# A decoder block on one core: ring sizes, quantiser instructions, bank choice and issue orders changed together

## The reference

```python
x = layernorm(x + attention(x))        # 16 heads of 32, causal, softmax in f32, biases
x = layernorm(x + cross(x, ctx))       # q, k from ctx (256 wide); A = softmax(q k^T) over 512; out = x @ A^T
x = layernorm(x + ffn(x))              # the line below

xq = clip(round(s * r), -128, 127) / s          # r = (x - mean) / sqrt(var + 1e-8), s = 127 / max|r| per row
ffn = (silu(xq @ sign(W_g).T) * (xq @ sign(W_u).T)) @ sign(W_d).T     # hidden width 2048
```

## Time and profile before

| what | value |
|---|---|
| median of three runs | 581.6 us |
| the profiled execution: its time, its span | 582.68 us, 580.9 us |
| TensorE (PE) busy | 550.0 us, 95% |
| VectorE (DVE) busy | 478.7 us, 82% |
| ScalarE (ACT) busy | 420.7 us, 72% |
| GpSimd (POOL) busy | 381.3 us, 66% |
| granted TensorE clock, mean | 0.989 |

### The profile page before, as it was taken

One profiled execution on the slowest core, in us unless ns is written; L12 is line 12 of the kernel. 1 busy time (PEld: TensorE's weight loads), 2 busy tenths in 40 slices (PEclk: granted clock), 3 DMA queues, 4 the chain that ended last, 5 costly groups with the idle time before them and its releaser, 6 DMA issues.

```text
span 580.9 us, 14215 instructions
## 1 busy us (share of the span) xinstructions
PE 550.0 (95%) x5324; PEld 356.2 (61%) x5324; DVE 478.7 (82%) x1252; ACT 420.7 (72%) x789; POOL 381.3 (66%) x409
## 2 busy tenths in 40 slices
...
GB/s 303 304 332 186 272 244 261 81 55 91 137 65 183 138 120 181 191 173 93 90 110 160 136 160 100 199 144 87 43 117 164 143 188 178 137 109 37 24 33 36
DMA packets 220516, 84.29 MB, mean 145 GB/s; under 512 B 207008, under 2 KB 211616, under 8 KB 218912
## 3 DMA queue, kind: packets, MB, share of 16 engines
...
...
...
## 4 chain that ended last, share of the span: by engine, by line
PE 47%; DVE 14%; POOL 4%; ACT 2%; issue 2%; DMA 2%; POOLq 0%; DVEq 0%; ACTq 0%; SPq 0%
PE ps_b L665 17%; PE ps_b L813 15%; PE ps_b L828 11%; DVE ps_b L1086 3%; PE ps_b L757 2%; PE ps_b L721 2%; POOL ph L1275 2%; DVE xq L1179 2%; DVE scaled L1176 2%; DVE bn L1019 1%; DVE rows L1214 1%; DMA x1T<-rhl 1%; DMA oT<-ohl 1%; ACT p L910 1%; POOL rstd L1250 1%
## 5 line engine op out<-in xcount | busy, mean ns | idle before, releaser
L1275 POOL TENSOR_TENSOR ph<-p,ph 128x768 f16<-128x768 f32 (+1 forms) x84 | 152.5, 1821 | 80.5 <-ACT ph L846 43.4
L910 ACT ACTIVATE p<-ps_b,tops 128x128 f32<-128x128 f32 (+3 forms) x256 | 120.2, 550 | 25.4 <-issue 15.3
L1086 DVE CUSTOM_DVE_ANT_0 ps_b<-ps_b,future 128x128 f32<-128x128 f32 (+3 forms) x256 | 117.6, 521 | 9.4 <-PE ps_b L721 9.2
L813 PE MATMUL ps_b<-xqT,sg 128*128 128x256 f16 x1024 | 119.1, 273 | 0.9 <-DVE rows L1214 0.6
L828 PE MATMUL ps_b<-sd,hp 128*128 128x512 fp8e4 x512 | 117.1, 379 | 0.0
L813 PEld LDWEIGHTS ps_b<-xqT,sg 128*128 128x128 fp8e4 x1024 | 98.4, 98 | 19.3 <-issue 1.8
L1271 POOL TENSOR_TENSOR hp<-gt,hp 128x512 f16<-128x512 f32 x64 | 74.1, 1161 | 38.9 <-ACT hp L846 38.7
L665 PE MATMUL ps_b<-xhl,wh 128*128 128x256 f16 x480 | 84.2, 275 | 1.0 <-POOL xhl L1275 0.5
L828 PEld LDWEIGHTS ps_b<-sd,hp 128*128 128x128 f16 x512 | 48.6, 98 | 54.8 <-issue 2.4
L846 ACT ACTIVATE ph<-p 128x768 f16<-128x768 f32 (+1 forms) x72 | 66.2, 926 | 3.5 <-DMA pt<-ph 3.3
L665 PE MATMUL ps_b<-xhl,wl 128*128 128x256 f16 x240 | 65.9, 275 | 0.0
...
## 6 DMA issues: line engine op xcount, KB each, us to landing
...
pt<-ph SPq DMA_TRANSPOSE x84, 4.3
...
```

Source lines behind the costliest of these rows:

```text
L813: ins = pe.matmul(ps[:, a * HALF:(a + 1) * HALF], sg[:, ("gg", "uu").index(name), c, ht * P:(ht + 1) * P], xqT[:, c, :], start=c == 0, sto ...
L910: ins = act.activation(p32[:, n % P32_SLOTS, to:to + keys], ps[:, col:col + keys], ACT.Exp, scale=-1.0, bias=tops[:, s % 2, g, j, qt % 2:q ...
L1086: ins = dve.tensor_tensor_reduce(scores, scores, future[:, S - width:S], EXP_SCALE, 3e38, ALU.add, ALU.min, tops[:, s % 2, g, j, qt % 2:qt ...
L1275: pool.tensor_tensor(out_, in_, hi, ALU.subtract).then_inc(signal, 1)
```

## The change

Five things change. `PH_SLOTS` goes from 3 to 4 and `PT_SLOTS` from 6 to 5. In `quantise` the step column `normed` is issued before `scaled` and `xq`, right behind the reciprocal. `scaled` and `xq` become `scalar_tensor_tensor` instructions whose second tensor is a constant column in SBUF (`levels`), read again for every element. The banks in `PE_ORDER` are chosen anew. All five orders are new; each has the same parts as before.

```diff
-CONSTS = 8
+CONSTS = 10
-P32_SLOTS, PH_SLOTS, PT_SLOTS, HP_SLOTS = 3, 3, 6, 6
+P32_SLOTS, PH_SLOTS, PT_SLOTS, HP_SLOTS = 3, 4, 5, 6
...
+        levels = sb("levels", [P, 2], F32)
...
                 dve.reciprocal(scale, step).then_inc(a_scale.sem, 1)
-                wait(dve, a_scale, s, t + 1)
-                wait_for(dve, wx_lo, 1)
-                dve.tensor_scalar(scaled[:, :], row, scale, MAGIC, ALU.mult, ALU.add).then_inc(a_magic.sem, 1)
-                wait(dve, a_magic, s, t + 1)
-                wait(dve, xqT_out[t], s, 0)
-                dve.tensor_scalar(xq[:, t, :], scaled[:, :], MAGIC, 127.0, ALU.subtract, ALU.min)\
-                   .then_inc(xq_out.sem, 1)
                 wait(dve, ln_rstd[2], s, t + 1)
                 wait(dve, invb_out, s - 1, 0)
                 dve.tensor_scalar(normed, step, root, DSCALE, ALU.mult, ALU.mult).then_inc(a_norm.sem, 1)
+                wait(dve, a_scale, s, t + 1)
+                wait_for(dve, wx_lo, 1)
+                wait_for(dve, consts, CONSTS)
+                magic, limit = (levels[:, i:i + 1].to_broadcast([P, D]) for i in range(2))
+                dve.scalar_tensor_tensor(scaled[:, :], row, scale, magic, ALU.mult, ALU.add).then_inc(a_magic.sem, 1)
+                wait(dve, a_magic, s, t + 1)
+                wait(dve, xqT_out[t], s, 0)
+                dve.scalar_tensor_tensor(xq[:, t, :], scaled[:, :], MAGIC, limit, ALU.subtract, ALU.min)\
+                   .then_inc(xq_out.sem, 1)
...
+                const(pool.memset(levels[:, 0:1], MAGIC))
+                const(pool.memset(levels[:, 1:2], 127.0))
```

The orders are long. These are the places of `PE_ORDER` around the `ib` parts of steps 0, 1, 3, 4 and 5 and around the second pair of `mx` in step 1, then the place of `DVE_ORDER` around the quantiser of step 3 (`n2` parts `n21.1.0` and `n21.1.1`):

```diff
-pv0.0.2.2@3 pv0.0.2.3@3 mx0.1.0.0@5,1,2,4 mx0.1.0.1@7,5,3,6 pv0.0.3.0@2 pv0.0.3.1@2 pv0.0.3.2@2 pv0.0.3.3@2
+pv0.0.1.3@0 qk0.1.3@1 tw0.0.2.0.0@5,4 va0.1.1@3 mx0.1.0.0@0,2,6,5 pv0.0.2.0@7 pv0.0.2.1@7 tw0.0.3.0.0@4,0 pv0.0.2.2@7
+pv0.0.2.3@7 mx0.1.0.1@1,3,4,2 pv0.0.3.0@0 pv0.0.3.1@0 pv0.0.3.2@0 pv0.0.3.3@0 tw0.1.0.0.0@7,6 qk1.0.0@5
...
-tw0.1.3.0.0@5,0 pv0.1.2.3@4 ib0@1 tw0.1.3.1.0@1,2 gg0.0.0@0 uu0.0.0@5 gg0.0.3@1 gg0.0.1@2 gg0.0.2@3 uu0.0.1@0
+va1.0.0@4 mx0.1.3.1@2,3,7,5 va1.0.1@6 pv0.1.2.0@0 pv0.1.2.1@0 tw0.1.3.0.0@1,2 pv0.1.2.2@0 pv0.1.2.3@0 ib0@3
...
-dn0.0.1.3@2 cp1.0@1 ib1@3 cp1.1@4 pv1.0.0.3@7 pv1.0.1.0@3 pv1.0.1.1@3 pv1.0.1.2@3 pv1.0.1.3@3 pv1.0.2.0@2 pv1.0.2.1@2
+pv1.0.0.2@2 pv1.0.0.3@2 dn0.0.1.0@3 dn0.0.1.1@3 ib1@0 dn0.0.1.2@3 mx1.1.0.0@6,7,4,2 cp1.0@5 cp1.1@0 dn0.0.0.3@1
...
-pv2.0.2.3@2 ib3@0 mx2.1.0.1@4,1,7,3 pv2.0.3.0@0 pv2.0.3.1@0 qk2.1.3@6 pv2.0.3.2@0 pv2.0.3.3@0 va2.1.0@1
+en2.1@1 en2.2@4 gg1.1.0@6 ib3@5 gg1.1.3@3 gg1.1.1@2 pv2.1.0.0@1 pv2.1.0.1@1 en2.3@5 pv2.1.0.2@1 pv2.1.0.3@1 gg1.1.4@6
...
-pv2.1.1.3@2 qk3.0.0@0 qk3.0.2@2 pv2.1.2.0@1 pv2.1.2.1@1 ib4@4 pv2.1.2.2@1 pv2.1.2.3@1 qk3.0.3@6 mx3.0.0.0@1,7,2,3
+mx2.1.3.0@0,1,2,7 va3.0.0@6 pv2.1.1.2@4 pv2.1.1.3@4 qk3.0.1@3 qk3.0.0@0 qk3.0.2@1 mx2.1.3.1@5,2,7,4 ib4@0 pv2.1.2.0@3
...
-dn2.0.1.2@6 pv3.0.2.1@1 pv3.0.2.2@1 pv3.0.2.3@1 pv3.0.3.0@3 pv3.0.3.1@3 pv3.0.3.2@3 ib5@7 dn2.0.1.3@6 cp3.0@4
+mx3.1.0.0@4,7,5,2 ib5@0 dn2.0.1.1@1 dn2.0.1.2@1 mx3.1.0.1@0,4,7,5 pv3.0.1.3@3 dn2.0.1.3@1 pv3.0.2.0@6 cp3.0@2
...
-xm1.1.0 xm1.1.1 mx2.0.3.0 mx2.0.3.1 mx2.0.3.2 n11.1.0 mx2.0.3.3 n21.1.0 n11.1.1 ov2.0.1 n21.1.1 mx2.1.0.0 mx2.1.0.1
+mx2.0.3.0 mx2.0.3.1 mx2.0.3.2 mx2.0.3.3 dn1.0.1 xm1.1.0 xm1.1.1 mx2.1.0.0 mx2.1.0.1 mx2.1.0.2 n11.1.0 mx2.1.0.3
+n21.1.0 qk2.1.1 mx2.1.0.4 mx2.1.0.5 mx2.1.0.6 mx2.1.0.7 n11.1.1 ov2.0.1 n21.1.1 qk2.1.2 qk2.1.3 ov2.0.2 va2.1.0
```

More of the change, by code:

```diff
@@ L96 @@
 SP_ORDER = """
[L97 to L106, removed]
@@ L113 @@
+tp3.1.1.1.1 ta3.3 tx3.0.0 tp3.1.2.0.0 tx3.0.1 tp3.1.2.0.1 tp3.1.2.1.0 tp3.1.2.1.1 tp3.1.3.0.0 tp3.1.3.0.1 tp3.1.3.1.0
+tp3.1.3.1.1 tq3.0.0 tq3.0.1 zn2.1.0 zn2.1.1 to3.1.0 to3.1.1 lr7 tx3.1.0 tx3.1.1 tq3.1.0 tq3.1.1 zn3.0.0 zn3.0.1
+zn3.1.0 zn3.1.1
 """
 PE_ORDER = """
-qp qk0.0.0@7 qk0.0.1@6 qk0.0.3@4 qk0.0.2@5 mx0.0.0.0@6,7,3,2 cp0.1@1 cp0.0@0 va0.0.0@5 va0.0.1@6 bv@1
-mx0.0.1.0@5,4,2,0 en0.2@6 en0.1@1 tw0.0.0.0.0@3,7 en0.0@5 en0.3@4 qk0.1.0@2 tw0.0.1.0.0@7,3 pv0.0.0.0@5 pv0.0.0.1@5
-pv0.0.0.2@5 pv0.0.0.3@5 va0.1.0@0 qk0.1.1@3 pv0.0.1.0@5 pv0.0.1.1@5 mx0.0.2.0@6,1,7,2 va0.1.1@0 qk0.1.2@6
```

351 lines of the change are left out of this document (180 added, 171 removed).

## The result

The changed kernel takes 588.03 us (median of 5 runs, 586.59 to 589.09); the kernel before, beside it on the same chip, 581.93 us (581.37 to 584.47). The ratio is 1.0093, 95% interval 1.0067 to 1.012: slower by 0.9%, where the prediction had 578.4 us and a range that ended at 585.0. In what follows "+5.4 us" and the like is (ratio - 1) x 583 us, since each run has its own runs of the kernel before on its own chip; the interval of such a difference is 0.8 to 1.6 us to each side. Busy times, waits and clocks come from one profiled execution of each kernel, which can lie up to 3 us from the median (run 15).

What follows compares the result with a forecast made beforehand. TensorE, busy 550.0 of 580.9 us, was taken as the bound, so only closing its gaps pays. Terms -4.0 - 2.0 - 1.6 - 1.0 + 2.4 + 0.5 + 2.5 = -3.2 us gave 578.4 us from 581.6, range 572.5 to 585.0.

Steps and rivals of the forecast that it cites:

- Banks: In front of the `ib` transposes: new banks and the earlier column remove most of TensorE's 5.5 us of waits, -4.0 us.
- step 3: Block maxima placed ahead of step 3's quantiser end TensorE gaps and the half clock behind them, -2.0 us.
- step 1's scores: `mx0.1.0.0` no longer waits for the division of `pv0.0.1`, since other TensorE work stands in between, -1.6 us.
- rings: Fourth `ph` slot ends ScalarE's waits, taken as 0; five `pt` slots shorten the distance for transposes, +0.5 us.
- rest of the orders: Remaining long gaps of TensorE are drawn anew and new ones appear, +2.5 us, bounds -2 and +6.
- the 4.05 us: TensorE's gap in front of `mx0.1.0.1`, behind the low halves of `tw0.0.3`: expected to stay, 0, bounds -4 to +2.
- the 1.5 us for `qk` halves: TensorE's wait at `mx1.1.3.0`, which gets other banks: -1.0 us, bounds 0 and -1.5.
- The quantiser's two instructions: `scaled` and `xq` as two-tensor instructions lengthen VectorE's work: +2.4 us at the end, bounds -3.9 and +5.3.
- Rival 1: Quantiser decides: VectorE keeps all stretching, `xq` lands later and `gg` waits for `xqT`; 585.8 us, chance 0.20.
- Rival 2: The repeated column brings no stretching of `scaled` and `xq`, -3.9 in place of +2.4; 572.1 us, chance 0.14.
- Rival 3: TensorE's gaps only move, freed banks meet the same busy VectorE, 8.6 us of gains come back; 581.6 us, chance 0.24.
- the signs named for "right": `ib` waits below two us, no clock drop near step 3's quantiser, VectorE busier by some 5 us, `pv` waits at most 1 us.

Runs made afterwards that it cites:

- run 15: Changed kernel with the one-tensor quantiser form, plus an extra two-tensor instruction (scalar_tensor_tensor) ahead of `scaled` in every tile: 600.59 us, ratio 1.0286.
- run 3: Changed kernel with `scaled` and `xq` back as one-tensor instructions; orders, rings and column as changed: 577.37 us, ratio 0.9904.
- run 13: Kernel before with the column first and other banks for three `ib` parts (ib0, ib1, ib3): 579.17 us, ratio 0.993.
- run 2: Kernel before with only the column `normed` moved in front of `scaled`: 580.07 us, ratio 0.995.
- run 6: Changed kernel with the one-tensor form and the old rings (three `ph` slots, six `pt` slots): 600.04 us, ratio 1.0285.
- run 1: Kernel before with only `scaled` and `xq` turned into two-tensor instructions: 589.98 us, ratio 1.0119.
- (8): Kernel before with the rounding left out, `xq` written by one `tensor_scalar` from the rows: 574.89 us, ratio 0.9866.
- (5): Kernel before with an added `tensor_reduce` over 384 columns of the row ahead of `scaled` in every quantiser call: 587.8 us, ratio 1.0076.
- run 12: Kernel before with an added 128x384 `tensor_reduce` in `add_down`, behind the down projection's add to the rows: 587.14 us, ratio 1.0079.
- run 9: Changed kernel with the one-tensor form, plus a 128x512 `tensor_reduce` ahead of `scaled` in every tile: 586.54 us, ratio 1.0071.
- run 4: Changed kernel with the whole old quantiser, one-tensor form and column last: 579.93 us, ratio 0.995.

## Why the prediction was wrong

**Banks, step 3, step 1's scores, rings, rest of the orders**: -4.0 - 2.0 - 1.6 - 1.0 + 0.5 + 2.5 = -5.6 us. Run 3 is the changed kernel without the quantiser's form, and measured -5.6 us. That the sum meets to a tenth is luck at least in part, since the terms were not measured one by one and those that were came out otherwise. Column and other banks together gave -4.1 us in the old orders (run 13), step 3's episode included, where the two steps said -6.0. And 2.9 of it came from the column alone, with VectorE 3.3 us less busy, which the step had not counted. The episode of step 3 went, but the column alone does it in the old orders (run 2), where the forecast gave it to the new place of the maxima; the clock stayed at 1.00 from 115 to 440 us, which includes the 305 us of the earlier trace rows. It came back in step 5, the "one more gap" that the step allowed for, with the long form and not without it (run 3). Step 1's scores: the 1.6 us in front of `mx0.1.0.0` are gone, but 1.3 us stand inside `tw0.0.3`, which writes a bank of `mx0.1.0.0`; the 4.05 us became 2.4, where no gain was taken, now behind ScalarE's exponential and not the low halves. Of the 1.5 us for `qk` halves, in front of `mx1.1.3.0`, 0.7 us at most are left anywhere at that line. The rings: the wait of `pv` for transposes is 1.4 us in three, a little over the "at most 1 us" named; but the fourth slot, taken at 0, carries these orders, which lose 22 us with the old rings (run 6). The rings' two terms, 0 and +0.5, have no run of their own, and they did not see what the orders rest on.

**The quantiser's two instructions** is the step that failed: +2.4 us taken, 11.0 us measured in the new orders (run 3 against the changed kernel), 6.9 us in the old ones (run 1), both above the upper end of +5.3. Of its two factors the second, the share of VectorE's time that reaches the end, was wrong in both sets of orders; the first, VectorE's time itself, in the new ones only.

The first: +10.0 us at the two lines after the change (+11.6 over run 3), where the upper bound was +7.2; in the old orders +6.4 us (run 1), inside it. The price of an undisturbed instruction was taken from lines that read PSUM (0.68 us); with both inputs in SBUF and float32 written it is 0.752 us, 0.07 us more in each tile. And "all of it stays" was no upper bound for the stretching: it went from 12.5 to 14.0 us, and from 10.9 us in run 3, whose orders are the same. In run 1 it fell to 10.4 us (33.5 less 23.1), so it hangs on which GpSimd instruction each tile meets; that a longer pair must meet more of them is not shown. The earlier trace rows had shown the mechanism, a VectorE instruction that waits for GpSimd, and the reading took it only as a reason for the upper end. GpSimd's own waits, 7 us of busy time, had no term at all.

The second, the share that reaches the end, was taken from the chain: 19.8 of 27.1 us, 73% as the most, and then half of that because TensorE "has other work ready". The runs give, per microsecond of VectorE's busy time:

| edit | orders | VectorE, us | time, us | ratio of both |
|---|---|---|---|---|
| rounding left out (8) | old | -14.4 | -7.8 | 0.54 |
| reduction at the quantiser (5) | old | +7.1 | +4.4 | 0.62 |
| reduction in `add_down` (12) | old | +6.8 | +4.6 | 0.68 |
| two-tensor form (1) | old | +6.1 | +6.9 | 1.13 |
| reduction (9 over 3) | new | +10.7 | +9.7 | 0.91 |
| two-tensor form (after over 3) | new | +11.6 | +11.0 | 0.95 |
| two-tensor pad (15 over 3) | new | +22.0 | +22.3 | 1.01 |

Nothing like a third. In this kernel VectorE, at 82% and with an order written out by hand, is nearly as good as a bound: its list hands back banks to TensorE all along it, and a delay at the quantiser (runs 5, 9) or behind the down projection (run 12) moved the rest. The clock is the smaller part of it: 1.7 of the 11.0 us of the form, and nothing in run 12. The new orders pass on nearly all of a delay, the old ones a little over half of it, as long as GpSimd isn't held as well. The difference between the two sets rests on the reduction runs, 0.91 and 0.62 with an uncertainty of some 0.15 and 0.2, so that the new orders are more tight is likely and not shown.

**Rival 1** was the mechanism that held, and its time, 585.8 us, is 2.2 us short of what was measured; its chance was put at 0.20. It was held down by the sentence that only 0.6 us of waits at `gg` and `uu` stood on VectorE. That was a wrong test: the delay hardly shows at the quantiser's own reader (L815 waits 2.1 us and 1.9 without it) but as waits for what stands behind the quantiser in VectorE's list, the maxima, the halves of `qk` and the divisions, as in step 5 above. So its sign and size held, and its way to the end, through `xq` and `gg`, did not. **Rival 2** is refuted by the maxima of 2.48 and 2.50 us. The rule of the Trainium skill that the prediction quoted (page "SBUF — State Buffer", section "Who interferes with whom") does not say whether a column read again for each element counts as an SBUF input. The rows of step 1 and step 2 above are as they would be if it does, the one 0.80 us longer than alone, the other holding a 0.19 us instruction for 0.73 us; but the first alone would not tell, since the one-tensor form was stretched too. The same section of the Trainium skill says that `tensor_scalar` in a mode that uses both ports contends and that `tensor_reduce` on this chip never does; run 9 agrees with both, 0.687 us at most for the one, means of 0.64 and 1.04 us for 0.48 and 0.43 of the other. **Rival 3** is refuted by run 3. Its sign, waits outside the fill not less than before but at other lines, did appear (28.7 us for 25.0), and the signs named for "right" appeared as well: the `ib` waits below 2 us, no drop of the clock in step 3, VectorE up by more than 5 us. So the signs did not tell the forecast from its rivals, and only taking the form out did.

Still open: how the 2.9 us of run 4 divide among banks, orders and rings. The new orders lose 22 us with the old rings, and no run has the old orders with the new ones; only the banks of the `ib` parts were tried by themselves, +1.7 and -1.2 us around run 2.
